# Moving five squares and a bias share onto VectorE in a macaron block (feed-forward, attention, feed-forward)

## The reference: what is computed

```python
x = x + 0.5 * ffn(layernorm(x), W_fc, W_proj)
x = x + attn(layernorm(x), Wk, bk, Wka, bka, Wv, bv, gamma, beta)
x = x + 0.5 * ffn(layernorm(x), W_fc, W_proj)

# ffn
h = square(relu(x @ W_fc.T))                      # 128 -> 512
y = h @ W_proj.T                                  # 512 -> 128
mem = 0
for _ in range(5):                                # spikes
    mem = 0.9 * mem + y - (mem > 1)
    spikes += (mem > 1)
return spikes / 5

# attn
h = layernorm(x) * gamma + beta
keys, values = h @ Wk.T + bk, h @ Wv.T + bv
w = exp((keys @ Wka.T + bka) / sqrt(128))
w = w / cumsum(w)
return cumsum(w * keys) * values
```

## Time and profile before

| | |
|---|---|
| median of 3 runs | 151.65 us (150.67 to 152.0) |
| the profiled execution, whole time | 150.15 us |
| its span in the profile | 148.3 us |
| PE busy | 142.2 us (96%) |
| PEld busy | 126.5 us (85%) |
| DVE busy | 126.3 us (85%) |
| ACT busy | 128.5 us (87%) |
| POOL busy | 96.5 us (65%) |
| granted TensorE clock | full in all 40 slices |

### The profile page before, as it was taken

How to read it: one execution, slowest core, us unless ns; L and a number is a source line. 1 busy time by engine, 2 the same in 40 slices (tenths; PEclk the granted TensorE clock), 3 DMA queues, 4 the chain that set the end, 5 groups by cost and what they waited for, 6 DMA issues and landing times.

```text
span 148.3 us, 3010 instructions
## 1 busy us (share of the span) xinstructions
PE 142.2 (96%) x945; PEld 126.5 (85%) x945; DVE 126.3 (85%) x437; ACT 128.5 (87%) x255; POOL 96.5 (65%) x142
## 2 busy tenths in 40 slices
PE   7899999999999999999999999999899999999990
PEld 7699898889889889988988989888789898979790
DVE  3994478689699999999989999999999999464674
ACT  3376979899999998979999999799798997978861
POOL 1448134968899928993999899979953954450200
PEclk9999999999999999999999999999999999999999
DMA  4975000000000000000000001000020011120222
GB/s 139 260 201 162 7 0 0 0 0 7 0 0 0 4 4 0 0 0 0 4 0 2 0 20 55 2 0 0 0 73 4 26 44 39 37 71 0 71 71 71
DMA packets 10510, 5.09 MB, mean 34 GB/s; under 512 B 1152, under 2 KB 10496, under 8 KB 10496
## 3 DMA queue, kind: packets, MB, share of 16 engines
q1 hardware_dynamic: 9808, 4.53, 10.6%
q10 hardware_dynamic: 688, 0.39, 0.9%
HBM read 2.82 MB, written 2.10 MB: 33 GB/s over the span
## 4 chain that ended last, share of the span: by engine, by line
PE 68%; DVE 14%; ACT 8%; issue 4%; DMA 3%; POOL 2%; ACTq 1%; DVEq 0%
PE work L1003 28%; PE hidden L924 8%; PE hidden L928 8%; PE hidden L925 7%; PE work L937 3%; DMA proj_raw<-in_L_ffn_W_proj_dram 3%; ACT signs L520 2%; PE att_work L1034 2%; PE att_value L1058 2%; DVE stats_att L602 2%; ACT square L497 2%; PE att_work L924 2%; PE att_work L928 2%; PE att_work L925 2%; DVE weight_sum L766 2%
## 5 line engine op out<-in xcount | busy, mean ns | idle before, releaser
L1003 PE MATMUL work<-proj_t,square 128*128 128x128 f32 x480 | 61.7, 276 | 0.1
L1003 PEld LDWEIGHTS work<-proj_t,square 128*128 128x128 f32 x480 | 59.0, 192 | 2.9 <-POOL square L425 0.5
L520 ACT ACTIVATE signs<-work 128x512 uint8<-128x512 f32 x73 | 41.3, 620 | 5.3 <-PE work L1003 5.3
L492 ACT ACTIVATE relu<-hidden 128x512 f32<-128x512 f32 x64 | 38.0, 626 | 0.0
L497 ACT ACTIVATE square<-relu 128x512 f32<-128x512 f32 x53 | 35.5, 670 | 0.3
L924 PE MATMUL hidden<-in_hi,fc_lo 128*128 128x512 f32 (+1 forms) x66 | 27.5, 417 | 0.1
L928 PE MATMUL hidden<-in_lo,fc_hi 128*128 128x512 f32 (+1 forms) x66 | 25.7, 389 | 0.0
L925 PE MATMUL hidden<-in_hi,fc_hi 128*128 128x512 f32 (+1 forms) x66 | 25.4, 385 | 0.0
L404 POOL TENSOR_TENSOR rstd<-var_eps,minus_half 128x4 f32<-128x4 f32 x15 | 15.3, 1021 | 14.6 <-DVE neg_mean L615 14.6
L410 POOL TENSOR_SCALAR normed_att<-x_att,neg_mean_att,rstd_att 128x128 f32<-128x128 f32 x32 | 18.3, 581 | 0.8
L675 DVE TENSOR_TENSOR in_lo<-work,in_hi 128x512 fp32r<-128x512 f32 x15 | 10.2, 678 | 9.1 <-ACT in_hi L488 9.0
(11 more groups left out here) (117 smaller groups left out, 251.7 us busy)
## 6 DMA issues: line engine op xcount, KB each, us to landing
x_first<-_attn_hidden_states_dram SPq DMA_DIRECT2D x7, 256.0 KB, 4.2
out_dram<-x_out SPq DMA_DIRECT2D x7, 256.0 KB, 2.2
out_dram<-x_out SPq DMA_DIRECT2D x4, 64.0 KB, 1.5
x_first<-_attn_hidden_states_dram ACTq DMA_DIRECT2D x1, 128.0 KB, 2.7
x_first<-_attn_hidden_states_dram SPq DMA_DIRECT2D x1, 128.0 KB, 2.4
fc_raw<-in_L_ffn_W_fc_dram SPq DMA_DIRECT2D x1, 128.0 KB, 2.7
fc_raw<-in_L_ffn_W_fc_dram ACTq DMA_DIRECT2D x1, 128.0 KB, 3.0
proj_raw<-in_L_ffn_W_proj_dram SPq DMA_DIRECT2D x1, 128.0 KB, 3.6
```

What stands on the lines that cost most here:

```text
L492: nc.scalar.activation(relu[j.lane][:, c, :], bank_of_hidden(j, c)[:], ACT.Relu).then_inc(relu_made[j.lane], 1)
L520: nc.scalar.activation(signs[j.lane][:, k, :], work[j.lane][:], func, bias=bias, scale=scale).then_inc(signs_made[j.lane], 1)
L1003: last = nc.tensor.matmul(work[j.lane][:, tokens], square[j.lane][:, c, tokens], proj_t[:, c, :], start=(c == 0 and t == 0), stop=(c == NC ...
```

## The change

Two edits are made together.

**Beta's share.** The two matmuls of L1100 and their semaphore go. `beta` is loaded as one row of 128 values repeated over all 128 partitions (64 KB in place of 0.5 KB, at the same place in SyncE's order). At the end of step 0 VectorE multiplies the unturned `Wk` and `Wv` by it, two products of 128x128. In step 1 it sums each product along its rows, one `tensor_reduce` of 128x256 to 128x2, and adds the biases to the sums. TensorE no longer waits for `vectors`.

**A second square on VectorE.** In jobs 0, 1, 2, 12 and 13 the third chunk's square (chunk 2) goes from ScalarE to VectorE. On VectorE it stands behind the second sum of job `i-1`, the same place at which the last job has its squares.

```diff
 DVE_SQUARES = [(0,), ()]
+FF_ONLY_JOBS = (0, 1, 2, 12, 13)
+FF_ONLY_DVE_SQUARES = (0, 2)
...
+        if i in FF_ONLY_JOBS:
+            self.dve_squares = FF_ONLY_DVE_SQUARES
...
-        vectors = sb("vectors", [P, 5])
+        vectors = sb("vectors", [P, 4])
+        beta_rows, beta_products = sb("beta_rows", [P, P]), sb("beta_products", [P, 2, P])
+        beta_sums = sb("beta_sums", [P, 2])
...
-            for k, v in enumerate((bk, bv, bka, gamma, beta)):
+            for k, v in enumerate((bk, bv, bka, gamma)):
                 sp.dma_start(vectors[:, k:k + 1], v.rearrange("(p a) -> p a", a=1)).then_inc(vectors_loaded, 16)
+            sp.dma_start(beta_rows[:], beta.partition_broadcast(P)).then_inc(vectors_loaded, 16)
...
                 dve.wait_ge(vectors_loaded, 16 * 5)
+                for a in range(2):
+                    nc.vector.tensor_tensor(beta_products[:, a, :], att_raw[:, a, :], beta_rows[:],
+                                            ALU.mult).then_inc(beta_multiplied, 1)
                 nc.vector.tensor_scalar(att_w[:, 0:2, :], att_t[:, 0:2, :], vectors[:, 3:4], ATT_GAMMA_SCALE,
...
                 dve.wait_ge(fold_mm, 1)
-                dve.wait_ge(beta_mm, 1)
...
-                nc.vector.tensor_tensor(kv_bias[:], att_value[:, 0:2], vectors[:, 0:2], ALU.add).then_inc(kv_bias_made, 1)
+                dve.wait_ge(beta_multiplied, 2)
+                nc.vector.tensor_reduce(beta_sums[:], beta_products[:], AXIS.X, ALU.add).then_inc(beta_summed, 1)
+                dve.wait_ge(beta_summed, 1)
+                nc.vector.tensor_tensor(kv_bias[:], beta_sums[:], vectors[:, 0:2], ALU.add).then_inc(kv_bias_made, 1)
...
                 for j in feed_forward(i):
                     if j.is_last:
                         ff_dve_square(j, 1)
-                        ff_dve_square(j, 2)
+                    ff_dve_square(j, 2)
...
                     pe.wait_ge(att_copied, 1)
-                    pe.wait_ge(vectors_loaded, 16 * 5)
                     nc.tensor.matmul(att_value[:, P:2 * P], att_raw[:, 0, :], att_t[:, 2, :], start=True,
                                      stop=True).then_inc(fold_mm, 1)
-                    for a in range(2):
-                        last = nc.tensor.matmul(att_value[:, a:a + 1], att_t[:, a, :], vectors[:, 4:5], start=True,
-                                                stop=True)
-                    last.then_inc(beta_mm, 1)
```

More of the change, by code:

```diff
@@ L291, in macaron_kernel @@
         fc_turned, proj_turned, att_turned = sem("fc_turned"), sem("proj_turned"), sem("att_turned")
-        beta_mm = sem("beta_mm")
+        beta_multiplied, beta_summed = sem("beta_multiplied"), sem("beta_summed")
         fc_hi_made, fc_ready, proj_ready = sem("fc_hi_made"), sem("fc_ready"), sem("proj_ready")
```

## The result

The changed kernel took 152.1 us (median of 20 runs, 150.98 to 153.04), the kernel before, beside it on the same chip, 150.86 us (20 runs, 150.16 to 152.36). The ratio is 1.0077 with an interval of 1.005 to 1.0104: 0.8% slower, inside what I had called no change, but measurable with this many runs. The forecast of 152.0 us is met partly by luck: it stood on a median of three runs (151.65) that 20 runs put 0.8 us lower, so the difference forecast was +0.37 us and the one measured +1.2 us. Part of that 1.2 us is a difference in how many executions started late, which the next paragraph explains: among the early starts alone the medians differ by 0.9 us (151.33 against 150.45), among the late ones by 0.45 (152.47 against 152.02).

A forecast was written before the change was run, and what follows sets the result against it. TensorE was taken to bound step 1 and VectorE the late attention steps. +0.37 (step 3) + 0.20 - 0.20 (jobs 12 and 13) = +0.37 us on the 151.65 us median gave 152.0 us, range 150.5 to 153.3.

The forecast's parts named there:

- Beta's matmuls, -0.45 us: Step 1 on TensorE: removing the four records of beta's matmuls saves 0.45 us.
- rival 1: VectorE's additions fit into idle time, so both TensorE savings stay: -0.65 us, 151.0 us; chance 0.22.
- `in_lo` of job 1, +0.28: Step 0's new VectorE work makes job 1's `in_lo` late, stalling TensorE at L928 by 0.28 us.
- `in_lo` of job 2, +0.88: Step 1's square and row sums make job 2's `in_lo` late: TensorE stalls 0.88 us, standing at +0.71.
- Absorbed in step 3, +0.37 left: TensorE already waited about 0.5 us there; +0.37 us remains, through job 2's first square and GpSimd to L1034.
- The middle as one block, 0: All of the middle follows from step 3, so the +0.37 us sum stays unchanged until step 12.
- The last point of the prediction: Sign of being wrong: the middle gives a distance back or adds to it, being nearly full on four engines.
- `in_lo` of job 13, +0.20: Job 12's square moves job 13's `in_lo` by 0.61 us, stalling TensorE at L928 by 0.20 us.
- Job 13's square, -0.20: Fits VectorE's idle time; chunk 3's wait for ScalarE goes, job 13's contractions take 1.95 us, not 2.15: -0.20 us.
- The second, GpSimd slowed: Rival: squares contending for SBUF slow GpSimd's four tiles on the attention chain by 0.46 us: 152.5 us; chance 0.12.
- The third, the repeated row: Rival: beta's repeated row lands late, VectorE waits before the first product; landing at 14.1 gives 153.9 us; chance 0.09.
- The margin of 1.8 us: Beta's load lands at about 10.4 us, its first reader is due at about 12.2: hidden by 1.8 us.

The follow-up runs named there:

- e1: Only beta's share moved to VectorE, no squares, against the kernel before; its profile gains 0.44 us by step 2, nothing left by step 3.
- e6: Beta's share in VectorE's idle time of step 1, row loaded early with its own semaphore, no extra squares; 0.44 us gained by step 2, nothing left by step 3.
- e7: e6 with job 13's extra square alone on VectorE; differs from e6 by 0.02 us in net span.
- e12: e6 plus job 1's third-chunk square on VectorE, behind the attention weights and ahead of job 3's statistics; 150.01 us against 150.47 for the kernel before, ratio 0.9971.
- e5: The changed kernel run once more, unaltered, against the kernel before; ratio 1.005.
- e8: The changed kernel with job 1's square left on ScalarE; net span 0.68 us less than e5, median not distinguishable from the kernel before.
- e3: The changed kernel with beta's repeated row issued before the third batch of x and the small vectors; 0.09 us of net span against e5.
- e9: The changed kernel with twelve one-column memsets added in VectorE's idle time at the start; ratio 1.005, net span 139.81 us.
- e4: Only the squares of jobs 12 and 13 moved, against the kernel before; loses 0.20 us at step 14, gets back 0.09 by step 15.
- e10: e6 plus job 1's third-chunk square on VectorE, right behind the first square; contraction of chunks 2 and 3 takes 1.95 us, no overall time given.
- e2: Only the five squares moved, beta's matmuls left on TensorE, against the kernel before; loses nothing in the first steps, no overall time given.

## Why the prediction was right, and where it was not

- **Beta's matmuls, -0.45 us.** Right: 0.38 us where there were 0.82, and -0.44 at step 2 in e1, e6 and e7, where no stall follows. But I had them *stay* in rival 1 and never asked what else would bind. ScalarE's square of job 1's last chunk is due just where TensorE needs it, so without the other edit the saving ends in step 2 (e6; e12 shows it kept).
- **`in_lo` of job 1, +0.28.** Changed kernel +0.16, e5 +0.34 (by the step 2 starts, with -0.44). Right in place and size.
- **`in_lo` of job 2, +0.88.** Measured 0.84 in the changed kernel (10.68 to 18.53 takes 7.85 us where it took 7.01) and 0.93 in e5. Right; what it is made of, the wait for the relu with the square behind it, shows in VectorE's rows (0.71 us of idle ahead of 20.60), and e8 and e12 undo it.
- **Absorbed in step 3, +0.37 left.** +0.17 and +0.42 in the two profiles, +0.30 in e3 and +0.23 in e9. Right in kind, and the sizes lie on both sides of the forecast. GpSimd's `rstd_att` starts 0.23 (changed) and 0.48 us (e5) later from T on, so the detour through the first square of job 2 decides, as forecast, and one of the two waits at L1046 is left.
- **The middle as one block, 0.** Wrong: +0.31 us for the pause in VectorE's stream. I had looked at four engines' load there and left the pause at a fixed place of the instruction stream out, although has one (0.23 us "issue" at L829). The last point of the prediction named the middle as what could break it.
- **`in_lo` of job 13, +0.20.** Measured +0.18 (119.78 - 112.36 = 7.42 us against 7.24), e4 +0.20. Right.
- **Job 13's square, -0.20.** Measured -0.08 (126.97 - 119.78 = 7.19 us against 7.27), and e7's step is 0.03 us shorter than e6's. This is a step that failed. The sixteen matmuls did fall to their undisturbed time, and I wrote that what is late next, GpSimd's square of job 14, is unchanged. It is not. "Fits in idle time of VectorE" was true for VectorE only; GpSimd's tiles and square hang behind it, and 0.13 us of the 0.20 went there. I had also taken for this wait. In the changed kernel the same wait of 0.3 us is still in the list, at 40.47 us in step 4; that row was never job 13's, and the earlier trace rows alone carried the term.

```profile
131.21 1.95 PE L1015 MATMUL work<-proj_t,square 128*128 128x128 f32 x16
...
136.07 2.05 PE L1015 MATMUL work<-proj_t,square 128*128 128x128 f32 x16
```

The first of these rows of the changed kernel answers to the second of the earlier trace rows. From its successor, L936 at 132.91, to the next contraction at 136.07 it takes 3.16 us. Before it took 3.03.

The net sum by measured terms: +0.17 to step 4, -0.04 to step 8, +0.31 to step 13, +0.18, -0.08, and nothing behind: +0.54 us in the profile of the changed kernel. The forecast had +0.37, with the pause missing and job 13's gain too large. e5, the same kernel, has +0.80; what makes its `in_lo` stalls 0.18 and 0.09 us longer I have not found. The timed difference of 1.2 us in the first comparison is larger than either, while e5, the same kernel, measured 0.5 us (1.005). Part of the first is the share of late starts, which fell the other way in e5's comparison (at 151.5 us or more 2 of 12 against 7 of 35); among the early starts alone the first comparison has the 0.9 us named above. Nothing in these runs ties that share to the change, and what is left between 0.9 us and the profile's 0.54 has no cause shown.

Of the rivals, the first (additions hidden) fails on both waits for the relu, as its "against" said. The second, GpSimd slowed, has its mechanism but not its place: the attention tiles at step 3 are not slower (1.76 us for four, before 1.84), the four tiles of job 15 are, from 1.73 to 2.26 us (2.27 in e7). That agrees with the Trainium skill (GPSIMD Engine Reference, Key points), by which VectorE instructions with two SBUF inputs contend with GpSimd: the row sum and `x_out` beside them have two, and `in_lo`, which overlaps the quick tiles in e6, reads one of its inputs from PSUM. The third, the repeated row, did not come true but was near: my term for the load, 3.7 us, was too small. The row landed at about 12.3 us, 5.7 us after its issue and not 3.7, right where the rival began to count. Its first reader stood at 12.46 in e5. The margin of 1.8 us was down to 0.1.

## What to carry to other kernels

When an edit takes time off the bounding engine, find the *second* arrival at the same wait first: here ScalarE's square was only just in time, so the saving was worth 0.03 us of net span alone (e6) and 0.38 us with that square moved as well (e12). When work is moved to an engine that works in order, its place in the queue matters more than its length. The same 0.69 us square, right behind the first square, where its relu was not there yet (e10), and ahead of the statistics (e12), makes a difference of 0.96 us at step 3 and 0.56 us at the end. And "idle time" of an engine is only free if nobody waits for what is queued behind it: follow the statistics to GpSimd before calling a hole a hole.

## What the runs showed of the hardware

- **A row of 512 bytes repeated to 128 partitions landed late, and the loads beside it too, in one of two places of the queue.** Issued at 6.64 us, it took 5.7 us to landing in the changed kernel and in e5 (5.3 in e1), against 3.7 for an ordinary load of 64 KB issued at 3.71, and the seven 256 KB loads took 6.4 us in the median (6.5 in e5) instead of 4.2. Issued at 4.19 us, ahead of one 256 KB load and the small vectors (e3), it took 3.8, and they 4.2 again. An ordinary 64 KB load in the late place was not run, so how much is due to the repetition is open.
- **VectorE's instruction stream pauses at a fixed count.** 0.17 to 0.22 us of idle time "issue", at the 320th record of VectorE's trace in seven profiles; it falls on another operation when instructions are added far ahead of it. What it costs depends on what stands there: 0.43 us on VectorE at a short row sum, 0.27 to 0.31 at a `var_eps` or `neg_mean` (e1, e2, e6), 0.13 to 0.15 beside a row sum (e8, e10, e12), nothing visible when moved by twelve instructions (e9). An edit that adds three to six instructions early can pay for it 60 us later.
- **TensorE starts at either of two spacings, and how long the slow one lasts differs from execution to execution.** Matmuls of 256 columns came every 0.21 us until 10.4 us in the changed kernel (0.99 us of idle time ahead of the first transposes) and until 9.1 us in e12 (0.72 us), but every 0.12 us in e2 (1.24 us) and in the kernel before (none). 256 columns in 0.21 us are 1.2 a nanosecond, the rate of the 1.2 GHz level; 256 in 0.12 us are 2.1, nearly that of 2.4 GHz. The Trainium skill (TensorE: Matmul & The Clock Gate, Part 1) has the two levels and says that the number of slow matmuls at the start varies from run to run of one kernel; the spacings agree. The granted clock of the profile, 1.00 in both stretches, does not show it:

```profile
4.40:8.81 4.41, 3.96 (x26) 3.49 (x27) 4.09 (x21) 1.94 (x6) 1.28 (x2) 1.00 0.79 215
```

```profile
5.37:10.99 5.62, 5.45 (x27) 5.02 (x28) 3.39 (x17) 2.00 (x6) 0.87 (x2) 1.00 0.65 151
```

These are the windows of the kernel before and of the changed one from the first transposes to T; the last three columns are the granted clock, the DMA share and GB/s.
